# Two small sums, one transfer and three products moved in the first microseconds of a GRU kernel

## The reference, cut to what matters

```
def step(h, inp):
    x_t, prop = inp
    comb = jnp.concatenate([x_t, h], axis=-1)
    z = jax.nn.sigmoid(comb @ Wz + bz)
    r = jax.nn.sigmoid(comb @ Wr + br)
    comb2 = jnp.concatenate([x_t, r * h], axis=-1)
    h_cand = jnp.tanh(comb2 @ Wh + bh)
    h_new = (1.0 - z) * h + z * h_cand
    h_next = jnp.where(prop, jnp.tanh(h_new @ Wp + bp), h_new)
    return (h_next, h_new)
...
x = x + gru(x, cond_1024, Wz, bz, Wr, br, Wh, bh, Wp, bp)
```

## Time and profile before

| | |
|---|---|
| median of 3 runs | 1042.19 us (1041.93 to 1043.15) |
| the profiled execution, its own time | 1043.28 us |
| its span, first to last instruction | 1041.3 us |
| TensorE busy (matmuls) | 1034.5 us, 99% |
| VectorE busy | 882.1 us, 85% |
| ScalarE busy | 776.1 us, 75% |
| mean granted TensorE clock | 1.000 |

### The profile page before, as it was taken

The page is one execution under the profiler, slowest core; times in us unless marked ns, Lnnn a source line. Parts: engine busy times, 40 slices in busy tenths (PEclk is TensorE's granted clock), DMA queues, the critical chain, the costliest instruction groups (busy, mean ns, idle before and its releaser), DMA issues.

```text
span 1041.3 us, 48291 instructions
## 1 busy us (share of the span) xinstructions
PE 1034.5 (99%) x20826; PEld 953.8 (92%) x20826; DVE 882.1 (85%) x2929; ACT 776.1 (75%) x1789; POOL 0.2 (0%) x4
## 2 busy tenths in 40 slices
PE   9999999999999999999999999999999999999998
PEld 4578999999999999999999999999999999999998
DVE  6978888898888998888988888988889988776665
ACT  5877777787777777777777777877777777665565
POOL 0000000000000000000000000000000000000000
PEclk9999999999999999999999999999999999999999
DMA  9312211001111001111011110011110000000001
GB/s 326 114 62 66 83 54 43 31 15 43 43 43 43 22 25 43 43 43 42 5 42 43 43 43 23 23 43 43 43 43 17 30 23 23 23 24 24 24 4 44
DMA packets 38485, 47.27 MB, mean 45 GB/s; under 512 B 2176, under 2 KB 34048, under 8 KB 37888
## 3 DMA queue, kind: packets, MB, share of 16 engines
q1 hardware_dynamic: 38000, 44.12, 12.6%
q10 hardware_dynamic: 272, 0.07, 0.0%
HBM read 27.40 MB, written 16.78 MB: 42 GB/s over the span
## 4 chain that ended last, share of the span: by engine, by line
PE 96%; DVE 2%; DMA 1%; SPq 0%; issue 0%; ACT 0%; DVEq 0%
PE acc L1346 37%; PE x_acc L1260 33%; PE acc L1354 16%; PE x_acc L1150 8%; DMA x_part<-wz_dram 1%; PE x_acc L1281 0%; ACT gate L585 0%; DVE x_lo L890 0%; DVE gate L1037 0%; DVE gate L1055 0%; DVE q_split L1026 0%; DVE q_split L1042 0%; DVE h_split L1105 0%; SPq L415 0%; SPq L412 0%
## 5 line engine op out<-in xcount | busy, mean ns | idle before, releaser
L1260 PE MATMUL x_acc<-x_hi,win_hi 128*128 128x256 f16 x1092 | 297.7, 273 | 0.0
L1260 PE MATMUL x_acc<-x_lo,win_hi 128*128 128x256 f16 x1092 | 297.7, 273 | 0.0
L1260 PE MATMUL x_acc<-x_hi,win_lo 128*128 128x256 f16 x1092 | 297.6, 273 | 0.0
L585 ACT ACTIVATE gate<-gate,unscale 128x128 f32<-128x128 f32 (+1 forms) x303 | 124.2, 434 | 129.0 <-DVE gate L1055 80.5
L591 ACT ACTIVATE gate<-acc,unscale 128x128 f32<-128x128 f32 (+1 forms) x397 | 127.6, 370 | 95.3 <-PE acc L1346 93.5
L1346 PE MATMUL acc<-h_split,wrec_lo 128*128 128x64 f16 x4096 | 180.2, 193 | 0.4 <-DVE h_split L1105 0.4
L1354 PE MATMUL acc<-h_split,wrec_hi 128*128 128x128 f16 x2608 | 172.3, 219 | 0.2 <-DVE h_split L1026 0.2
L551 ACT ACTIVATE x_part<-x_acc,bias,part_unscale 128x256 f32<-128x256 f32 x312 | 154.6, 560 | 17.8 <-PE x_acc L1260 17.7
L1346 PE MATMUL acc<-q_split,wrec_hi 128*128 128x64 f16 x3968 | 160.2, 193 | 0.0
L1346 PEld LDWEIGHTS acc<-h_split,wrec_lo 128*128 128x128 f16 x4096 | 155.0, 98 | 5.5 <-issue 0.6
L1354 PEld LDWEIGHTS acc<-h_split,wrec_hi 128*128 128x128 f16 x2608 | 148.2, 98 | 0.3 <-DVE h_split L1026 0.3
(11 more groups left out here) (147 smaller groups left out, 1508.3 us busy)
## 6 DMA issues: line engine op xcount, KB each, us to landing
out_dram<-x_blk SPq DMA_DIRECT2D x30, 512.0 KB, 3.2
x_blk<-x_dram SPq DMA_DIRECT2D x24, 512.0 KB, 3.8
x_blk<-x_dram SPq DMA_DIRECT2D x3, 1024.0 KB, 9.2
x_part<-wz_dram SPq DMA_DIRECT2D x4, 256.0 KB, 7.2
x_part<-wh_dram SPq DMA_DIRECT2D x4, 256.0 KB, 7.0
x_part<-wr_dram SPq DMA_DIRECT2D x1, 1024.0 KB, 11.4
x_part<-wz_dram SPq DMA_DIRECT2D x1, 1024.0 KB, 13.6
x_part<-wh_dram SPq DMA_DIRECT2D x1, 1024.0 KB, 17.3
```

The lines of the kernel that those rows point to most:

```text
L585: nc.scalar.activation(gate[g][:, half], gate[g][:, half], func, scale=unscale[:, g:g + 1]).then_inc(gate_ready[g], 1)
L1260: mm = nc.tensor.matmul(in_halves(x_acc[bank][:])[:, j], weights[g][:, slot_w, k, j * P:(j + 1) * P], in_halves(values[m % 2][:, slot_x, : ...
```

## The change

Three edits. The sum of x's magnitudes moves from behind fp32 product (1, 2) to behind (2, 0), two products later, and the sum of Wz's magnitudes from behind (2, 2) to behind (2, 3), one later. The load of Wr's quarter 2 is issued ahead of Wz's quarter 0 and not behind it. `AHEAD` goes from 32 to 35: three more of block 1's products stand ahead of step 0, and three fewer in steps 0 to 7. No instruction is added or removed.

```
-AHEAD = 32
+AHEAD = 35
...
             for k in (1, 2, 3):
                 load_first_x(k)
-            load_in(Z, 0)
             load_in(R, 2)
-            for k in (1, 2, 3):
+            for k in range(KC):
                 load_in(Z, k)
             load_in(R, 3)
...
-                    if (k, j) == (1, 2):
+                    if (k, j) == (2, 0):
                         reduce_x_magnitude(0)
-                    if (k, j) == (2, 2):
+                    if (k, j) == (2, 3):
                         pe.wait_ge(mag_ready[WIN + Z], KC)
                         for n in range(KC):
                             mm = add_magnitude(mag_sum(WIN + Z), mag_win[:, n:n + 1])
```

## The result

| | before | changed |
|---|---|---|
| median | 1042.51 us (22 runs, 1041.93 to 1043.70) | 1043.97 us (22 runs, 1043.30 to 1044.84) |
| ratio | | 1.0014, interval 1.0008 to 1.0020 |
| profiled execution | 1043.28 us, span 1041.3 | 1043.30 us, span 1041.3 |

The changed kernel is 1.46 us slower, 0.14%. That is within the 0.2% that I took for "the same", of the sign that I forecast, and nearly three times the forecast +0.5; the time lies 0.07 above the range. (Of the gap between 1042.7 and 1043.97, 0.3 is that three runs of before gave 1042.19, and more of them 1042.51.) The two profiled executions show the same span, though the medians differ by 1.46: that of before lies 0.8 above its kernel's median, and that of after is the fastest of its kernel's 22. So the difference of the kernels can't be read from this pair; single stretches can.

The account below looks back on a forecast made before the run. TensorE was taken to bound the kernel (96% of the span). Terms: 0 (start) + 0.54 (step 3) + 0 (steps 1, 3, 6) = +0.5 us on the median 1042.19, forecast 1042.7, range 1041.4 to 1043.9.

Parts of the forecast that it names:

- edit 2, "against 19.66, nothing is won": Start: gate Z's first product, held by ScalarE's first copy, comes at about 19.65 against 19.66 before; gain 0.
- Edit 1, the loads: Loads before step 0: exchanged, Wr 2 should land at 11.19 and Wz 0 at 11.87, in order of issue.
- Rival 3: Loads: Wr 2 lands no earlier than before, at 11.87; 0.7 lost at the start, 1.2 with step 3; 12%.
- the rule beside it: Loads: the Trainium skill says completion isn't first in, first out per issuing engine; if the order failed, +1.2 us.
- Edit 2, TensorE: Start: (2, 0) runs 11.48 to 12.34 after waiting for Wr 2; fp32 part ends at 19.1, not 19.59.
- Edit 2, ScalarE: Start: splits of x at 12.85, 0.85 later; prop_bias 15.34, splits of Wz 16.38, first copy 18.84, done 19.5.
- Edit 2, VectorE: Start: last two reductions (mag_win) done at 15.5, 0.4 later than 15.11.
- Edit 3, the count: Steps 2 and 3: step 2 gets two copies, step 3's sigmoid of R slides 0.66, TensorE stands still for 0.54.
- Edit 3, covers: Steps 1, 3 and 6, one product fewer each; step 7 has least room, at most 0.1; taken as 0.
- Rival 1: Start: gate Z's first product isn't held by the copy, so the start wins its 0.5; 1042.2; 14% alone.
- Rival 2: Step 3: no stall, with the start as forecast; 1042.2; 14% alone.
- Rival 4: Start: the clock falls to 1.2 GHz over eight fp32 calls, 6.9 more, 1049.6; 1%.

Follow-up runs that it names:

- e1: The changed kernel with AHEAD back at 32, so only the load order and the two later sums differ from before: 1043.11 us against 1042.61.
- e3: The kernel before with only the load of Wr 2 issued ahead of Wz 0: 1042.88 us against 1042.61.
- e4: The kernel before with both sums later, loads and AHEAD as they were: 1043.57 us against 1042.61.
- e5: The kernel before with x's sum behind (1, 3), one fp32 call later: +0.4 us against 1042.43.
- e6: The kernel before with x's sum behind (2, 0), Wz's sum left behind (2, 2): +1.1 us against 1042.43.
- e7: The kernel before with Wz's sum behind (2, 3), x's sum left behind (1, 2): +0.3 us against 1042.43.
- r10: The changed kernel measured a second time, nothing altered: 1043.96 us against 1042.64 for the kernel before.
- e2: The kernel before with AHEAD 35 alone: 1043.24 us against 1042.61.
- e14: The changed kernel with x's sum back behind (1, 2): 1043.35 us against 1042.45 for the kernel before.
- e15: The changed kernel with Wz 0 loaded ahead of Wr 2 as before: 1044.11 us, +1.7 against the kernel before.
- e8: The changed kernel with AHEAD 34 and not 35: 1043.10 us against 1042.43 for the kernel before.
- r9: The kernel before measured a second time, nothing altered: 1042.54 us against 1042.64.
- e12: The changed kernel with AHEAD 32, ScalarE's prop_bias and VectorE's low split of x's first quarter moved later: 1043.33 us against 1042.64 for the kernel before.
- e13: The changed kernel, AHEAD 35, with ScalarE's copy of group 17 moved from step 2 back to step 3: 1043.14 us against 1042.45 for the kernel before.
- e11: The changed kernel with AHEAD 34, ScalarE's prop_bias and VectorE's low split of x's first quarter moved later: 1043.36 us against 1042.64 for the kernel before.

## Why the prediction was wrong

The price splits at gate Z. Behind it the traces agree closely. From gate Z to the start of the last step it takes 1013.4 in the kernel before and in e1, e3, e4, e5, e6 and e7, all with `AHEAD` 32, and 1014.0 to 1014.1 in the changed kernel, r10, e2, e14 and e15, all with 35 and the second copy; e8, with 34, takes 1013.6. (r9, e12 and e13 are left out: they have the late holes of the last section, e11 and e12 the reordered lists.) So `AHEAD` costs 0.63, as step 3 shows, e8's 0.18, e13's nothing, and the rest of the time's difference is when gate Z starts. By the timed runs that is 0.5 (e1), 0.67 less 0.18 = 0.5 (e8), 0.7 (e13), 1.32 less 0.63 = 0.7 (r10) and 1.46 less 0.63 = 0.8 (changed): **0.6 to 0.7 for the start, 0.63 for `AHEAD`**, together 1.3, which agrees with 1.3 to 1.5. Alone, `AHEAD` cost 0.4 to 0.6 (e2).

**The step that failed: edit 2, "against 19.66, nothing is won", a start of 0.** It was taken as the start's value in every execution; measured it is +0.6 to +0.7. The mechanism was named right: ScalarE's list takes over as what gate Z waits for. What was wrong is the 19.66, the kernel before's own start, from which I took the difference. I read TensorE's 0.9 of waiting for x off one trace and took it as the kernel's, when the text itself said that this execution lay 1.1 above the median. Putting the forecast on the median didn't mend that, since the 19.66 stayed in it. Of the 17 traces that there are now, the kernel before's first has the latest last `mag_x` of all, 11.23; the others lie between 9.5 and 11.04. Six of the 17 have x's sum at its old place:

| trace, sum behind (1, 2) | last mag_x done | sum of x | gate Z | between |
|---|---|---|---|---|
| before, as predicted from | 11.23 | 11.28 | 19.66 | 8.38 |
| r9, before again | 10.96 | 11.09 | 19.40 | 8.31 |
| e2 | 11.04 | 11.09 | 19.46 | 8.37 |
| e3 | 9.99 | 11.31 | 19.41 | 8.10 |
| e7 | 10.28 | 10.81 | 19.04 | 8.23 |
| e14 | 10.94 | 11.00 | 19.23 | 8.23 |
| **sum behind (2, 0), Wz's behind (2, 3)** | | | | |
| after | 10.31 | 11.96 | 19.23 | 7.27 |
| r10, changed again | 9.84 | 12.41 | 19.69 | 7.28 |
| e1 | 10.88 | 12.81 | 20.09 | 7.28 |
| e4 | 10.73 | 12.39 | 19.66 | 7.27 |
| e8 | 9.72 | 12.07 | 19.35 | 7.28 |
| e13 | 9.99 | 12.21 | 19.48 | 7.27 |
| e15 | 9.51 | 12.84 | 20.12 | 7.28 |

Above, the sum takes place when the later of two is there, x's magnitude or TensorE (in e3 x had been ready for 1.3 when TensorE came, rows below); below, when TensorE has done two more calls of 0.86, in all seven. From then it is 7.27 to 7.28 in each, the two lists. The gain of 1.0 in the last column (8.1 to 8.4 against 7.28) is less than the 1.72 of the two calls, and the difference is made up only if TensorE would have waited 0.6 to 0.9 for x. In the trace I used it had waited 0.73; in e3 and e7 it didn't wait. The mean of gate Z's start is 19.37 above and 19.66 below, 0.3 apart in these few traces; the timed runs say 0.6 to 0.7.

```profile
8.65 1.34 DVE L791 TENSOR_REDUCE mag_x<-x_blk 128x1 bf16<-128x512 f32 x2 [1.19 <-DMA x_blk<-x_dram]
...
11.31 0.24 PE L1155 MATMUL acc<-mag_x,sum_over 128*128 128x1 bf16 x4
```

What a usual execution looks like can be estimated from the times. A profiled execution's time less its gate Z is 1023.5 on average with `AHEAD` 32 (before, e1, e3 to e7) and 1024.1 with 35 (after, r10, e2, e14, e15). Taken off the medians, 1042.51 and 1043.97, that puts gate Z at about 19.0 before and 19.9 changed (an estimate). So my 19.65 for the changed kernel was near: the seven traces have 19.66 in the mean, with the sum of x at 12.38 for the forecast 12.34. The 19.66 for the kernel before was some 0.7 too late. Of the 1.3 by which the forecast 1042.7 was missed, 0.3 is the median of three runs, 0.1 is step 3, and the rest is this start.

Point by point:

- **Edit 1, the loads.** Wr 2 and Wz 0 exchanged their landings, 0.7 apart; in all 17 traces the two land in the order of issue. Rival 3 didn't show; of the rule beside it in the prediction, that completion isn't first in, first out (the Trainium skill, DMA: Bandwidth & Descriptors, Queues, rings and completion order), these two transfers give no instance. The order alone cost 0.3 or nothing (e3).
- **Edit 2, TensorE.** (2, 0) had no wait for weights in the trace after: x was at hand, and 22 MATMULs ran through. The end of the fp32 part, forecast at 19.1, came at about 18.8 (eight MATMULs of 0.43 from 15.37), and the copy was the last thing needed, as I had it.
- **Edit 2, ScalarE.** From the sum to the first split of x 0.47 for the forecast 0.51; `prop_bias` at 2.47, splits of Wz at 3.53, first copy at 6.00 behind that split's start: forecast 2.49, 3.53, 5.99. The chain was right to 0.04.
- **Edit 2, VectorE.** The last `mag_win` at 15.19, forecast 15.5; with Wz's sum moved too it has no effect at gate Z, since the copy comes later. The hole before gate Z, forecast about half a microsecond, is 0.4 (18.8 to 19.23).
- **Edit 3, the count.** Two copies in step 2 and the wait for `q_split`: forecast 0.54, the trace shows 0.47 as a wait, with the products 0.63 late; the runs 0.4 to 0.7. The mechanism is right, confirmed by e13, where the copy stands elsewhere and nothing is lost, and by e8, where one copy is left and 0.18. The size was 0.09 too small: the room that I put at 0.12 was 0.03.
- **Edit 3, covers.** Steps 1, 3, 6 have one product fewer in e13 too, and by step 7 it has lost nothing. Costed at 0, found 0.
- **Rival 1** (the start wins 0.5) needs splits of x from 12.35; they came at 12.43 in the fastest execution and at 12.89 in r10. The sign that I had named for it, gate Z at 19.2, did appear in the first trace (19.23), but that comes from TensorE's early arrival in this execution (sum at 11.96); the copy held gate Z in all seven traces. Out. **Rival 2** is out by the row with 0.47. **Rival 4**, a fall of the clock, didn't show: the eight MATMULs behind the last hole still take 0.43 each, as before.
- **The range.** Its lower half hung on rivals 1 and 2, and its upper end on rival 3 alone. A case "TensorE arrives later than x" was missing, though x's landing and TensorE's arrival are two independent times and only one pair of them was on the page.

No version here beats the kernel before. Which comes first at its sum, x or TensorE, depends on the execution: TensorE waited 0.73 in the first trace, x waited 1.3 in e3, and in r9 they met within 0.1. The hole of 0.9 that the first trace seemed to offer was that of one execution. The one of 0.25 before Wz's sum comes back in r9 (0.2) and not in e3; moving that sum alone (e7, +0.3) won nothing.

## What to carry to other kernels

A place in an in-order list where an engine meets a load is a race between two times; read both from several executions before moving it, and look first at how far the profiled execution's own time lies from the median. A later place gives up the early case for good: the wait becomes fixed where it was only possible. When a count of work is moved by a few products, look at what is issued per whole group: 216 products brought a copy of 0.66 in front of the one instruction without room, and 215 didn't. And a stall of up to 0.16 doesn't show as a wait behind TensorE's modelled tail: compare the starts.

## What the runs showed that I had not expected

TensorE's pace at the start differs from one execution to the next. The first eight fp32 MATMULs have half the width, and ten weight loads around them take, in the trace of e3 and in that of after:

```profile
3.55 3.66 PEld L1280 LDWEIGHTS x_acc<-x_blk,win_hi 128*128 128x128 f32 x10
```

```profile
3.48 2.66 PEld L1280 LDWEIGHTS x_acc<-x_blk,win_hi 128*128 128x128 f32 x10
```

A microsecond apart, for the same instructions: they start 0.43 from one another at first and 0.215 later, and the pace doubles at about 4.1 (e4), 4.9 (after), 5.2 (before), 6.6 (e1) or 7.0 us (e3). That is the ratio of the 1.2 and the 2.4 GHz level, but the windows of e3 show a granted clock of 1.00 there as well (columns as in the earlier trace rows):

```profile
4.00:4.50 0.50, 0.50 (x2) 0.38 (x2) 0.43 (x1) 0.00 (x0) 0.00 (x0) 1.00 0.84 178
```

So that the clock is the cause is my guess; no row shows it. What is shown is its effect: TensorE's arrival at the sum moves by up to 0.85 (11.96 in after, 12.81 in e1, with the same calls and loads in front), and the changed kernel passes this on in full.

Late in the kernel three executions (r9, e12 and e13) have holes with no releaser, of which these are r9's; e12's chain has them at 954.91 and 970.14, e13's one of 0.10 at 954.87. By the chains 0.63, 0.68 and 0.28 are lost between step start and step start around there, and nothing in e1, e3 and e7:

```profile
954.77 0.19 issue
...
970.00 0.15 issue
```

What makes them is not known; they come in one trace of the kernel before and not in its other, so they belong to the spread and not to the change.
